# VectorE takes GpSimd's sums of x1's blocks, and hg is turned two steps later

## What is computed

```python
x = x + L0_ffn(L0_cond(x, lang))
x = x + L1_ffn(L1_cond(x, slot))

# L0_cond: x W^T + 2 * sum over 8 experts of gate_e * (x A_e^T) B_e^T,
#          gates = softmax of the top 2 of (x Wr^T + 5 * onehot(lang))
# L0_ffn:  the top-1 router's value times (y A^T) Bw^T, rank 8 * 16
# L1_cond: y = x W1^T + b1 + 2 * (x A_slot) B_slot, one slot for each batch
# L1_ffn:  y Wb^T + b + 2 * sum of top-2 gates * (y A1_e^T) B1_e^T
```

## Time and profile before

| | us |
|---|---|
| median of 3 runs | 526.1 |
| the profiled execution | 525.7 |
| its span, first to last instruction | 523.9 |
| TensorE busy | 483.9 (92% of the span) |
| VectorE busy | 341.3 (65%) |
| ScalarE busy | 154.1 (29%) |
| GpSimd busy | 112.0 (21%) |
| mean granted TensorE clock | 0.975 of full speed |

### The profile page before, as it was taken

The page is one execution under the profiler, slowest core; times in us unless marked ns, Lnnn a source line. Parts: engine busy times, 40 slices in busy tenths (PEclk is TensorE's granted clock), DMA queues, the critical chain, the costliest instruction groups (busy, mean ns, idle before and its releaser), DMA issues.

```text
span 523.9 us, 8531 instructions
## 1 busy us (share of the span) xinstructions
PE 483.9 (92%) x2911; PEld 438.3 (84%) x2911; DVE 341.3 (65%) x923; ACT 154.1 (29%) x339; POOL 112.0 (21%) x98
## 2 busy tenths in 40 slices
PE   5999999999999958998997998999799899899996
PEld 4987999999988858887987988888798798798895
DVE  3646755584768785676875677676777667763642
ACT  4445520322212542223222223223323223221310
POOL 2040000000001452124214115213321401510410
PEclk9989999999999987999999999899999899999998
DMA  7974728111103010611703423062060260300202
GB/s 242 348 240 156 228 91 162 41 41 41 46 35 86 3 22 3 81 53 49 83 0 103 62 22 103 13 70 87 16 80 15 87 80 4 102 2 1 95 2 81
DMA packets 88277, 40.29 MB, mean 77 GB/s; under 512 B 68487, under 2 KB 82321, under 8 KB 88110
## 3 DMA queue, kind: packets, MB, share of 16 engines
q1 hardware_dynamic: 87966, 39.25, 30.7%
q0 software_dynamic: 272, 0.56, 0.5%
HBM read 28.64 MB, written 11.16 MB: 76 GB/s over the span
## 4 chain that ended last, share of the span: by engine, by line
PE 48%; issue 24%; DVE 13%; POOL 8%; ACT 3%; DMA 2%; SPq 0%; POOLq 0%; DVEq 0%; ACTq 0%
PE banks L1350 13%; PE banks L1352 13%; PE banks L1351 13%; PE banks L1364 3%; PE banks L1345 3%; POOL x_raw L586 3%; DVE left L909 2%; POOL xTlo L586 2%; POOL left L586 2%; DVE G L909 2%; POOL x_raw L596 1%; ACT left L656 1%; DVE gbc L1006 1%; DVE b_acc L1181 1%; DVE x_raw L1069 1%
## 5 line engine op out<-in xcount | busy, mean ns | idle before, releaser
L1350 PE MATMUL banks<-G,left 128*128 128x460 f32 x224 | 89.9, 401 | 0.0
L1351 PE MATMUL banks<-G,left 128*128 128x460 f32 x224 | 84.5, 377 | 0.0
L1352 PE MATMUL banks<-G,left 128*128 128x460 f32 x224 | 83.8, 374 | 0.0
L586 POOL TENSOR_TENSOR xTlo<-x_raw,xThi 128x512 fp32r<-128x512 f32 x28 | 35.2, 1278 | 193.6 <-ACT xThi L656 193.6
L1350 PE MATMUL banks<-WbThi,ws_hi 128*128 128x460 f32 (+1 forms) x216 | 75.2, 348 | 0.5 <-DVE Mdir L909 0.5
L1352 PE MATMUL banks<-WbThi,ws_lo 128*128 128x460 f32 (+1 forms) x216 | 73.4, 340 | 0.0
L1351 PE MATMUL banks<-WbTlo,ws_hi 128*128 128x460 f32 (+1 forms) x216 | 73.1, 338 | 0.0
L656 ACT ACTIVATE left<-x_raw 128x512 fp32r<-128x512 f32 x64 | 38.7, 627 | 82.8 <-DVE x_raw L1069 28.9
L909 DVE SCALAR_TENSOR_TENSOR left<-x_raw,left 128x512 fp32r<-128x512 f32 x48 | 39.4, 835 | 18.3 <-ACT left L656 17.8
L1350 PEld LDWEIGHTS banks<-G,left 128*128 128x128 f32 x224 | 43.4, 194 | 5.1 <-DVE wzTlo L909 0.2
L1352 PEld LDWEIGHTS banks<-G,left 128*128 128x128 f32 x224 | 43.1, 192 | 4.8
(11 more groups left out here) (209 smaller groups left out, 1057.0 us busy)
## 6 DMA issues: line engine op xcount, KB each, us to landing
out_dram<-ybuf SPq DMA_DIRECT2D x15, 512.0 KB, 2.8
x_raw<-in_x_dram SPq DMA_DIRECT2D x56, 128.0 KB, 3.9
x_raw<-in_L_cond_W_dram SPq DMA_DIRECT2D x10, 512.0 KB, 5.3
wraw<-in_L_cond_W_dram SPq DMA_DIRECT2D x6, 512.0 KB, 4.5
wraw<-in_L_ffn_W_base_dram SPq DMA_DIRECT2D x4, 512.0 KB, 6.3
x_raw<-in_L_ffn_W_base_dram SPq DMA_DIRECT2D x4, 512.0 KB, 6.6
xin_first<-in_x_dram SPq DMA_DIRECT2D x1, 1024.0 KB, 8.4
x1T_dram<-xin_first SPq DMA_DIRECT2D x1, 1024.0 KB, 4.2
```

The costliest lines, as they stand in the source:

```text
L586: return gp.tensor_tensor(out_, a, b, ALU.subtract)
L1350: pe.matmul(out_, l[0], r[0], start=start, stop=False, **kw)
L1351: pe.matmul(out_, l[0], r[1], start=False, stop=False, **kw)
L1352: return pe.matmul(out_, l[1], r[0], start=False, stop=stop, **kw)
```

## The change

1. GpSimd's `s_sums` is gone; VectorE makes the four sums. Sums 0 and 1 stand after `a_part(q, ., 3)`, sum 2 after `s_part(q, ., 0)`, sum 3 in the next slot after `s_part(b, turn, 1)`.
2. S4 is written over the block (1,1) and not over (0,1). So half 0 of x_raw is free once the fourth sum is made, and SP loads half 0 of the next tile then, ahead of the rows E, and half 1 after `s34_lo`, as before.
3. VectorE's slot begins with `gates0(a)`; `s_part(b, turn, 1)` follows it. `turn_x(1)` moves from ahead of the `x1_add`s to the slot's end.
4. GpSimd's `xT_lo_part(a + 1)` waits for `hg_ready` of a, the S3 and S4 remainders for `hg_ready` of a+1, and `xT_lo_part(n)` for `wh_ready` of a+1.
5. On TensorE hg is turned after step 14 (20 in slot 0) and not 12, `add_lora0` stands at 17 and not 15, and what follows shifts by one step (by seven in slot 0, where `late` is 6) up to the turn of wz. The first two `lora`s of tile m+1 stand behind ffn0's groups 0 and 1 and not after step 42 (in slot 7, where there is no ffn0, after step 37).

```diff
 def slot_dmas(b, turn, last, more_x):
+                if more_x:
+                    sp.wait_ge(s_raw, b * 4 + 4)
+                    load_x(b * 2 + 4, 0, x_raw[turn])
                 if not last:
                     sp.wait_ge(z1_done, m + 2)
                     load_e(b + 1)
                 if more_x:
                     sp.wait_ge(s34_lo, b * 2 + 2)
-                    for half in range(2):
-                        load_x(b * 2 + 4 + half, half, x_raw[turn])
+                    load_x(b * 2 + 5, 1, x_raw[turn])
...
 # GpSimd
-            s_sums(0, 0)
             def slot(b, turn, has_a, has_n):
                 if has_a:
+                    gp.wait_ge(hg_ready, a + 1)
                     xT_lo_part(a + 1, 1, x_raw[1 - turn])
+                    gp.wait_ge(hg_ready, a + 2)
                 s_lo_part(b, turn, 0)
                 s_lo_part(b, turn, 1)
                 if has_n:
+                    gp.wait_ge(wh_ready, a + 2)
                     xT_lo_part(n, 0, x_raw[turn])
-                if has_a:
-                    s_sums(q, 1 - turn)
...
 # VectorE
+            s_sums(0, 0, (0, 1))
             s_part(0, 0, 0)
+            s_sums(0, 0, (2,))
             def slot(b, turn, has_a, has_n):
+                if has_a:
+                    gates0(a, q)
                 s_part(b, turn, 1)
-                if has_a:
-                    gates0(a, q)
+                s_sums(b, turn, (3,))
                 hs_part(m, 0)
...
-                if has_n:
-                    dve.wait_ge(x_in[1], b * 64 + 64)
-                    turn_x(1, x_raw[turn])
                 if has_a:
                     x1_add(q, 0, raw)
...
                     a_part(q, 1 - turn, 3)
+                if has_a:
+                    s_sums(q, 1 - turn, (0, 1))
                 y_c21(b)
                 y_c22(b)
                 if has_a:
                     as_part(q)
                     s_part(q, 1 - turn, 0)
+                    s_sums(q, 1 - turn, (2,))
                 y_c12(b)
+                if has_n:
+                    dve.wait_ge(x_in[1], b * 64 + 64)
+                    turn_x(1, x_raw[turn])
...
 # TensorE
-                main_to(12)
+                late = 6 if first else 0
+                main_to(14 + late)
                 if has_a:
                     turn_small(hg_ready, a + 1, pt_hg, hg[:, :], thg_done)
-                main_to(15)
+                main_to(17 + late)
                 if has_a:
                     add_lora0(a)
-                main_to(16)
                 turn_hs(m)
-                main_to(18)
+                main_to(19 + late)
                 adapter(m, 0)
                 turn_hs(m + 1)
-                main_to(20)
+                main_to(21 + late)
                 adapter(m + 1, 1)
...
-                main_to(21)
+                main_to(22 + late)
                 if has_a:
                     small0(a + 1, main_tile)
-                main_to(24)
+                main_to(24 + late)
...
                         main_to(39 + g)
-                main_to(42)
-                lora(m + 1, 1, 0)
-                lora(m + 1, 1, 1)
+                        if g < 2:
+                            lora(m + 1, 1, g)
+                if not has_a:
+                    lora(m + 1, 1, 0)
+                    lora(m + 1, 1, 1)
                 main_to(43)
```

More of the change, by code:

```diff
@@ L524, in slot_dmas @@
                     load_as(b + 1, True)
+                if more_x:
+                    sp.wait_ge(s_raw, b * 4 + 4)
+                    load_x(b * 2 + 4, 0, x_raw[turn])
+                if not last:
                     sp.wait_ge(z1_done, m + 2)
@@ L591, in xT_lo_part @@
                     sub(half_of(xT[1], h), raw_block(raw, half, h), half_of(xT[0], h).bitcast(F32)).then_inc(xT_lo, 1)
[L593 to L603, removed]
             def s_lo_part(q, turn, n):
@@ L607, in s_lo_part @@
                 gp.wait_ge(s_hi, q * 4 + 3 + n)
-                sub(left[:, 1, :], raw_block(x_raw[turn], 1 - n, n), left[:, 0, :].bitcast(F32)).then_inc(s34_lo, 1)
+                sub(left[:, 1, :], raw_block(x_raw[turn], 1, n), left[:, 0, :].bitcast(F32)).then_inc(s34_lo, 1)
             gp.wait_ge(x_turned, 1)
@@ L622, in _ @@
             gp.memset(Fbuf[:, :].bitcast(F32), 0.0).then_inc(memsets_done, 1)
-            s_sums(0, 0)
             def slot(b, turn, has_a, has_n):
-                a, n, q = b * 2 + 2, b * 2 + 4, b + 1
+                a, n = b * 2 + 2, b * 2 + 4
                 if has_a:
+                    gp.wait_ge(hg_ready, a + 1)
                     xT_lo_part(a + 1, 1, x_raw[1 - turn])
+                    gp.wait_ge(hg_ready, a + 2)
                 s_lo_part(b, turn, 0)
@@ L728, in s_part @@
                     act.wait_ge(p_done, q * 7 + 1)
-                i, j = ((1, 1), (1, 1), (1, 0), (0, 1))[nth]
-                hi_half(s_raw, q * 4 + (1, 3, 2, 4)[nth], left_of(turn)[name][:, 0, :], raw_block(x_raw[turn], i, j), s_hi)
+                j = (1, 1, 0, 1)[nth]
+                hi_half(s_raw, q * 4 + (1, 3, 2, 4)[nth], left_of(turn)[name][:, 0, :], raw_block(x_raw[turn], 1, j), s_hi)
             def keep_p1(b):
@@ L1080, in s_part, with s_sums @@
                 lo(left[:, 1, :], raw_block(x_raw[turn], 1, 1), left[:, 0, :]).then_inc(s12_lo, 1)
+            def s_sums(q, turn, nths):
+                raw = x_raw[turn]
+                A11r, A12r, A21r, A22r = (raw_block(raw, i, j) for i in range(2) for j in range(2))
+                for nth in nths:
+                    if nth == 0:
+                        dve.wait_ge(a_lo, q * 4 + 4)
+                        dve.tensor_tensor(A22r, A21r, A22r, ALU.add).then_inc(s_raw, 1)
+                    elif nth == 1:
+                        dve.tensor_tensor(A21r, A11r, A21r, ALU.subtract).then_inc(s_raw, 1)
+                    elif nth == 2:
+                        dve.wait_ge(s12_lo, q * 2 + 1)
+                        dve.tensor_tensor(A22r, A22r, A11r, ALU.subtract).then_inc(s_raw, 1)
+                    else:
+                        dve.wait_ge(s12_lo, q * 2 + 2)
+                        dve.tensor_tensor(A22r, A12r, A22r, ALU.subtract).then_inc(s_raw, 1)
             def add_y(tile, part, bank, base, ready):
@@ L1278, in slot @@
                 raw = x_raw[1 - turn]
-                s_part(b, turn, 1)
                 if has_a:
                     gates0(a, q)
+                s_part(b, turn, 1)
+                s_sums(b, turn, (3,))
                 hs_part(m, 0)
```

## The result

The changed kernel takes 509.94 us (median of 4 runs, 509.1 to 511.43) against 526.19 us; the ratio is 0.9695, 95% interval 0.9668 to 0.9723. The forecast was 509.2. The profiled execution took 509.24 us with a span of 507.4 us.

A forecast was written before the change was run, and what follows sets the result against it. TensorE, 92% busy, lost time waiting for hg (VectorE's gates colliding with GpSimd) and x1_add, and to half clock. 525.7 - 11.8 - 8.2 + 3.1 = 508.8 profiled, 509.2 us as median; range 501 to 518.

The forecast's parts named there:

- hg and the collision: Gates beside GpSimd's xT remainders: chain 4.4 us, 2.35 with GpSimd idle; TensorE's hg wait falls from 2.65–2.98 to 0.4.
- What bounds: Opening step: TensorE is busy 92%; it waits 24.4 us for hg and 11.5 for x1_add, and sometimes loses clock.
- The end of the slot: Step following VectorE's queue from ffn0's end: sums 0.6 us each, hg at 369.05, TensorE waits 0.4 us.
- hgTlo: Behind hg: S2's remainder, GpSimd's first xT remainder, then the fourth sum; TensorE waits 1.6 us, bounds 0.4 and 2.9.
- x1_sum and the loras: Two loras fill gaps behind ffn0's groups 0 and 1: x1_sum waits 14 and not 21, 0.75 us a slot.
- That saves 0.9 us a slot: The claimed saving from two loras filling ffn0's gaps; small0 starts 1.2 us earlier after ffn0's end.
- At nothing: Items costed at zero: SP's load order with 16 us of cover, GpSimd's second xT remainder, S3's remainder.
- Half 0 comes earlier: SP's earlier load of x's half 0, listed among the items costed at nothing.
- The five slots: Five steady slots of 40.65 us each: 203.3 instead of 215.1, -11.8 us.
- Slot 0: Gates at 194.8, a 3.2 us wait for wz and second hg together; 234.4 against 242.57, -8.2 us.
- Slot 7: hgTlo +1.6 in slot 6; slot 7 starts 1.5 us later as asraw's remainder comes late; together +3.1.
- The clock: No half clock counted after the change; rival that half the slots still drop: 516.0 us, chance 0.13.

The follow-up runs named there:

- a_sp: The changed kernel with both halves of x loaded behind s34_lo in SP's queue, as before, S4 keeping its new place: 557.98 us.
- b_lora: The kernel before, plus only the two loras behind ffn0's groups 0 and 1: 536.22 us, ratio 1.0177.
- a_hg12: The changed kernel with hg turned after step 12 and add_lora0 at 15, as before, in all slots, slot 0 too: 522.09 us.
- b_gates2: The kernel before, plus only GpSimd's first wait, so its xT remainders of tile a+1 begin behind hg: 508.37 us, ratio 0.9652.
- a_turnx: The changed kernel with turn_x(1) between x1_add(1) and x1_add(2): 503.42 us, ratio 0.9567.
- a_sum3: The changed kernel with the fourth sum behind hs and hgTlo in VectorE's queue: 499.97 us, ratio to before 0.9492.

## Why the prediction was right

**hg and the collision (steps "What bounds" and "The end of the slot"): right.** gac and gbc were slow through GpSimd: one wait on GpSimd alone took 18 us off. hg's wait was 0.17 to 0.34 us where 0.4 was forecast, but for the 1.84 of slot 3. VectorE's sums are 0.69 us each by their rows and 0.61 by their pitch, as taken.

**hgTlo: right.** 1.52 us against 1.6, with the order of the two engines as argued. Removing the cause removed it. The wait of 0.2 us for wh did not come.

**x1_sum and the loras: the waits were nearly right, the step was wrong.** 14 waits and 0.75 us a slot were forecast, 7 waits and 0.55 came. "That saves 0.9 us a slot" took a filled gap for time won. As VectorE's chain starts at ffn0's end, the time came back as waits for hg and hgTlo, and the second lora delays that end by 0.45 us. In the sum this did little harm only because I worked hg's and hgTlo's waits out from the lead that it gives TensorE.

**At nothing: wrong in part.** "Half 0 comes earlier" was costed at nothing. It does cost nothing, but it covers 48 us that the change would have cost without it (a_sp); a reader of that line would have left it out. The transpose did not wait for half 1, as forecast.

**The five slots:** 203.3 forecast, 201.7 measured. Two errors stand against each other: 0.6 us a slot less in small waits, and 1.56 us for VectorE's loop, which I had not seen because in the kernel before VectorE was idle 1.99 us at that point, where the other slots of the loop have 1.5 anyway.

**Slot 0:** hg at 194.8 and the pair's wait of 3.35 came as forecast (194.8, 3.2), but the half clock behind it, which I had left at none, makes 235.86 of 234.4. **Slot 7:** Mdir's wait 3.14 against some 3, with half clock behind it as well; from the sixth hg to the end 69.8 us against 66.2 before, +3.6 for +3.1.

**The clock** was counted at nothing: "no wait of over 1.7 us is left but one". That contradicts the prediction's own waits, as it forecasts one of 3.2 us in slot 0 and one of some 3 us ahead of slot 7. Both came, both with half clock, and cost 3.4 us. Slots 1 to 6 were clean, as forecast. In b_lora and a_hg12 the clock was the largest miss too.

**The total is closer than its parts, and that is luck:** five slots 1.6 us less than forecast, slot 0 1.5 more, slot 7 and the end 0.5 more. They leave 0.4 us, 509.24 against 508.8 for the profiled execution. It also took a fold as long as that of the trace before; S1's remainder ahead of slot 0 begins anywhere from 189.2 to 193.7 us in the traces of the other runs.

## What to carry to other kernels

Where VectorE's small operations last over 1 us beside GpSimd's large ones, first hold GpSimd back by one wait: here that alone gained as much as the whole change (b_gates2). Before filling another engine's gap, ask from which event its chain counts; filling ahead of that event delays the chain, and taking it back made one kernel 6 us faster (4.6 of them behind the fold) and the other 4 slower. And a wait put on one engine must be followed through to the DMAs that its results release.

## What the runs showed of the hardware

At its loop's turn VectorE does nothing new for 2.7 us after the y ahead of it, in three traces alike (2.71, 2.70 and 2.69 us in the changed kernel, a_turnx and a_sum3), with no releaser that the profile shows; written out, the gap is gone. It is no constant: in the kernel before, the next instruction begins 2.0 us after the y. One instruction of the old trip could fill a part, the transpose of 1.2 us. The Trainium skill, Runtime: NRT & Kernel Launch, section Instruction fetch mechanics, says that a taken branch out of the fetched pages stalls until the target is there. That agrees in kind; no run here shows a fetch.

TensorE's clock is not a matter of the longest wait. In the kernel before it fell after waits of 2.99, 2.65 and 2.65 us (slots 2, 3 and 5) and not after 2.70, 2.98 and 2.72 (slots 1, 4 and 6). In b_lora it fell with each wait of about 4 us. In a_hg12 it fell in slot 1 with two waits of 0.89 and 1.62 us and not in slot 2 with 1.07 and 1.60. A stretch that began at the end of the wait or behind it lasted about 3.4 us and cost 1.5 to 1.7. One that began over 1 us before the wait's end lasted longer: 7 us, with 2.5 lost, in slots 1, 3 and 5 of b_lora, and 10 us, with 2.9 lost, in slot 0 before. What of its history TensorE's clock follows stays open.
